# Order of the first chunks' splits, multiplies and condition groups in the prologue of a gated feed-forward kernel

## The reference

```python
scale = cond @ norm_w.T + 1.0
h = x * (scale[:, None, :] * rsqrt(mean(x * x) + 1e-6))
u = h @ up_w.T                        # 512 -> 2 * 2048
val, gate = split(u, 2)
h = val * gelu(gate)                  # exact gelu
hq = act_quant(h)                     # per row, 127 steps of its largest absolute value
wq = weight_quant(down_w)             # to -1, 0, 1 times a mean
x1 = hq @ wq.T + x
# adapter, whose two matrices depend on cond
Wd_b = Wd + 0.1 * (cond @ Wdd.T + bdd).reshape(B, 128, 512)
Wu_b = Wu + 0.1 * (cond @ Wdu.T + bdu).reshape(B, 512, 128)
out = x1 + relu(x1 @ Wd_b.T + bd) @ Wu_b.T + bu
```

## Time and profile before

| | us |
|---|---|
| median of 3 runs (lowest, highest) | 851.65 (851.64, 852.14) |
| the profiled execution's own time | 851.16 |
| its span in the trace | 849.1 |
| PE busy | 834.2 (98%) |
| DVE busy | 606.3 (71%) |
| ACT busy | 388.8 (46%) |
| POOL busy | 77.3 (9%) |

### The profile page before, as it was taken

How to read it: one execution, slowest core, us unless ns; L and a number is a source line. 1 busy time by engine, 2 the same in 40 slices (tenths; PEclk the granted TensorE clock), 3 DMA queues, 4 the chain that set the end, 5 groups by cost and what they waited for, 6 DMA issues and landing times.

```text
span 849.1 us, 11801 instructions
## 1 busy us (share of the span) xinstructions
PE 834.2 (98%) x3982; PEld 366.9 (43%) x3982; DVE 606.3 (71%) x904; ACT 388.8 (46%) x633; POOL 77.3 (9%) x79
## 2 busy tenths in 40 slices
PE   6899999999999999999999999999999999999998
PEld 4334444444444444444444444444444444444443
DVE  5998787989877765558776556668975664445986
ACT  5678887765454532237445542126433332224000
POOL 0463333302000000001000000000200000000100
PEclk9999999999999999999999999999999999999999
DMA  9879988666999843377899754436247444432232
GB/s 344 329 259 341 348 284 299 236 222 217 327 343 361 300 164 118 112 247 272 296 316 328 274 197 137 154 106 205 86 135 219 137 161 140 139 114 78 100 123 75
DMA packets 64426, 183.49 MB, mean 216 GB/s; under 512 B 7024, under 2 KB 8304, under 8 KB 64368
## 3 DMA queue, kind: packets, MB, share of 16 engines
q1 hardware_dynamic: 64080, 182.48, 61.7%
q10 hardware_dynamic: 288, 0.26, 0.1%
HBM read 152.31 MB, written 29.36 MB: 214 GB/s over the span
## 4 chain that ended last, share of the span: by engine, by line
PE 93%; DVE 1%; issue 0%; DVEq 0%
PE aux_ps L1182 10%; PE b_ps L1082 9%; PE b_ps L1084 9%; PE b_ps L1086 9%; PE a_ps L1082 6%; PE a_ps L1084 6%; PE a_ps L1086 6%; PE aux_ps L1137 6%; PE aux_ps L1233 3%; PE aux_ps L1224 3%; PE c_ps L1084 3%; PE c_ps L1082 3%; PE c_ps L1086 3%; PE e_ps L1082 3%; PE e_ps L1084 3%; PE e_ps L1086 3%
## 5 line engine op out<-in xcount | busy, mean ns | idle before, releaser
L1589 DVE SCALAR_TENSOR_TENSOR h_ring<-v_sb,unscale,gelu 128x512 f32<-128x512 f32 x63 | 51.0, 809 | 102.1 <-ACT gelu L885 54.8
L861 ACT ACTIVATE b_ps<-a_ps 128x512 f32<-128x512 f32 x63 | 36.7, 582 | 141.7 <-PE a_ps L1086 141.6
L1082 PE MATMUL b_ps<-t_mov,u_l 128*128 128x512 f16 x252 | 95.5, 379 | 0.5 <-DVE c_ps L1550 0.5
L1086 PE MATMUL b_ps<-t_mov,u_l 128*128 128x512 f16 x252 | 95.5, 379 | 0.0
L1084 PE MATMUL b_ps<-t_mov,u_l 128*128 128x512 f16 x252 | 95.5, 379 | 0.0
L1613 DVE TENSOR_TENSOR hmax<-gelu,hmax 128x512 f32<-128x512 f32 x120 | 82.8, 691 | 7.7 <-ACT gelu L891 2.6
L1182 PE MATMUL aux_ps<-h_ring,wq 128*128 128x512 f16 x384 | 84.8, 379 | 0.0
L753 POOL PARTITION_ALL_REDUCE yscale<-hmax x8 | 17.8, 2265 | 601.9 <-DVE hmax L1613 601.2
L895 ACT ACTIVATE gelu<-h_ring 128x512 f32<-128x512 f32 x64 | 40.3, 629 | 56.6 <-DVE h_ring L1589 56.6
L891 ACT ACTIVATE gelu<-h_ring 128x512 f32<-128x512 f32 x64 | 40.2, 629 | 52.5 <-DVE h_ring L1599 52.4
L1599 DVE SCALAR_TENSOR_TENSOR h_ring<-b_ps,unscale,gelu 128x512 f32<-128x512 f32 x64 | 47.9, 749 | 18.8 <-PE b_ps L1086 18.7
(11 more groups left out here) (225 smaller groups left out, 1622.1 us busy)
## 6 DMA issues: line engine op xcount, KB each, us to landing
w_ring<-in_Wdu SPq DMA_DIRECT2D x64, 512.0 KB, 6.1
w_ring<-in_Wdd SPq DMA_DIRECT2D x56, 512.0 KB, 6.7
u_l<-ul_dram SPq DMA_DIRECT2D x48, 512.0 KB, 4.6
u_e<-ue_dram SPq DMA_DIRECT2D x48, 384.0 KB, 3.1
h_ring<-in_up_w SPq DMA_DIRECT2D x16, 512.0 KB, 6.3
x_sb<-in_x SPq DMA_DIRECT2D x8, 1024.0 KB, 8.0
res<-in_down_w SPq DMA_DIRECT2D x16, 512.0 KB, 7.5
ul_dram<-u_l SPq DMA_DIRECT2D x15, 512.0 KB, 5.3
```

The source lines that it names most:

```text
L1082: pe.matmul(ps[:, :], weight(n, p, 0, k), hi, start=fresh and k == 0, stop=False, skip_group_check=True)
L1086: mm = pe.matmul(ps[:, :], weight(n, p, 1, k), hi, start=False, stop=k == 1, skip_group_check=True)
L1589: dve.scalar_tensor_tensor(out=h_slot(n)[:, TB:TS], in0=val[:, :], scalar=unscale[:, s // 2, j:j + 1], in1=gelu2[:, :], op0=ALU.mult, op1= ...
```

## The change

It changes orders and no work. No instruction and no transfer is added or taken out. The names are those above.

- ACT: the early groups' copies are interleaved otherwise. Group 0's is in front of `t_high(0, B21)`, 1 and 2 behind it, and 3 and 4 around `row_sums(3)`. `u_high(1, 0)` and `u_high(1, 1)` come in front of `t_high(0, T1)`, and `u_high(1, 2)` and `seed_b(1)` in front of `t_high(0, T3)`.
- PE: group 0 in front of `spread_rs(1)`, group 2 in front of the B21 products, groups 3 and 4 around `bounds(1, 2)`, and group 7 in front of P7 of quad 1.
- DVE: `exponents(1, 2)` and `u_scale(1)` in front of T1. T1 and T2 back to back. `u_low(1, 0)` and `u_low(1, 1)` in front of `t_low(0, T1)`. `multiply2(0)` ahead of `t_low(0, T2)` and ahead of `multiply1(0)`. `u_low(1, 2)` in front of T3, `u_low(1, 3)` in front of `t_low(0, T3)`, and `u_scale(2)` behind it. `slot_empty(0)` stays written in both multiplies of quad 0.

```diff
--- before.py
+++ after.py
@@ -935,30 +935,32 @@
             t_high(0, B11)
             u_high(0, 2)
             row_sums(2)
+            stage_group(0)
             t_high(0, B21)
-            stage_group(0)
             stage_group(1)
+            stage_group(2)
             t_high(0, B12)
             t_high(0, B22)
             gate1(0)
-            stage_group(2)
+            stage_group(3)
             row_sums(3)
-            stage_group(3)
-            t_high(0, T1)
-            t_high(0, T2)
+            stage_group(4)
             u_high(1, 0)
             u_high(1, 1)
+            t_high(0, T1)
             gate2(0)
-            stage_group(4)
+            t_high(0, T2)
             stage_group(5)
+            u_high(1, 2)
             stage_group(6)
+            seed_b(1)
             t_high(0, T3)
-            u_high(1, 2)
             u_high(1, 3)
             for n in range(1, NQ):
                 s, j = divmod(n, NP)
                 last = j == NP - 1 and s + 1 < NSB
-                seed_b(n)
+                if n > 1:
+                    seed_b(n)
                 if last:
                     t_high(s + 1, B11)
                 if j == 0:
@@ -1253,21 +1255,22 @@
             stat1(1)
             first_product(a_ps[0], True, False, B11).then_inc(s_p[1], 1)
             first_product(b_ps[0], True, True, B11).then_inc(s_p[5], 1)
+            adapter_group(0)
             spread_rs(1)
-            adapter_group(0)
             adapter_group(1)
+            adapter_group(2)
             first_product(a_ps[0], False, False, B21).then_inc(s_p[2], 1)
             first_product(b_ps[0], False, True, B21).then_inc(s_p[4], 1)
-            adapter_group(2)
             adapter_group(3)
             pe.wait_ge(s_ms, 2)
             bounds(1, 2, e_ps).then_inc(s_total, 1)
+            adapter_group(4)
             pe.wait_ge(s_xs, 2 * KD)
             first_product(c_ps, True, False, B12).then_inc(s_p[6], 1)
             first_product(b_ps[1], True, True, B12)
             first_product(c_ps, False, False, B22).then_inc(s_p[3], 1)
             first_product(b_ps[1], False, True, B22).then_inc(s_p[7], 1)
-            for g in range(4, EARLY - 1):
+            for g in range(5, EARLY - 1):
                 adapter_group(g)
             for n in range(NQ):
                 if n:
@@ -1279,9 +1282,13 @@
                     if n > 1:
                         product(n - 1, 4)
                     product(n, 2)
+                    if n == 1:
+                        for g in groups_of_quad(n):
+                            adapter_group(g)
                     product(n, 7)
-                for g in groups_of_quad(n):
-                    adapter_group(g)
+                if n > 1:
+                    for g in groups_of_quad(n):
+                        adapter_group(g)
                 if stat_of_quad(n) is not None:
                     pe.wait_ge(s_p5sb, n)
                     stat(stat_of_quad(n))
@@ -1738,22 +1745,22 @@
             x_scaled(1)
             t_low(0, B12)
             t_low(0, B22)
-            moving_sum(0, T1)
             dve.wait_ge(s_total, 1)
             exponents(1, 2, e_ps)
             u_scale(1)
+            moving_sum(0, T1)
+            moving_sum(0, T2)
+            u_low(1, 0)
+            u_low(1, 1)
+            t_low(0, T1)
+            multiply2(0)
+            t_low(0, T2)
+            u_low(1, 2)
+            moving_sum(0, T3)
+            multiply1(0)
+            u_low(1, 3)
+            t_low(0, T3)
             u_scale(2)
-            moving_sum(0, T2)
-            t_low(0, T1)
-            u_low(1, 0)
-            t_low(0, T2)
-            moving_sum(0, T3)
-            u_low(1, 1)
-            multiply1(0)
-            multiply2(0)
-            t_low(0, T3)
-            u_low(1, 2)
-            u_low(1, 3)
             aux_ready(dve, "bounds", 0)
             exponents(3, 3, bank("bounds", 0))
             u_scale(3)
```

## The result

| | median, us (lowest to highest, runs) | ratio to before, 95% interval |
|---|---|---|
| before | 850.70 (850.05 to 852.14, 20) | |
| changed | 852.62 (851.95 to 854.90, 20) | 1.0023 [1.0017, 1.0029] |
| changed, measured again (e10, before 850.92 beside it) | 852.46 (11 runs) | 1.0016 [1.0007, 1.0025] |

The change makes the kernel 1.9 us slower, 1.5 in the repetition. The forecast was 2.06 us. The median that was forecast, 853.7, is 1.1 us above the measured one, and 0.95 of that is the base: it started from the 851.65 of three runs, and 20 runs of the kernel before gave 850.70. The profiled execution of the changed kernel took 852.54 us, its span is 850.5. The profiled executions of two experiments, e5 (4150 us) and e7 (1984 us), are not used, and both kernels were measured again as e11 and e9.

The account below looks back on a forecast made before the run. DVE's queue up to `seed_c(2)` sets P7(2), and PE is the bound from there. 1.65 + 1.26 - 0.48 (old idle gone) - 0.80 + 0.45 = +2.08, by the schedule +2.06, on 851.65 gives 853.7 us; range 851.3 to 854.9.

Parts of the forecast that it names:

- The groups on PE and ACT: Early groups fill PE's idle times, P1(1) is ready at about 37.2 instead of 39.51; costed at nothing in the sum.
- Step 1: DVE up to T2: POOL's sums of chunk 2 start sooner and slow DVE less, a gain of 0.80 us (0 to 1.43).
- Step 2: DVE at `multiply2(0)`: waits for the moves of groups 0 and 1, behind tile 15, until 37.70, a wait of 1.65 us.
- Step 3: DVE at `u_low(1, 3)`: waits for ACT's `u_high(1, 3)`, which stands behind `t_high(0, T3)`, a new wait of 1.26 us.
- Step 4: DVE at low half T3: now beside POOL's sums of chunk 3 and slowed by 0.45 us (0 to 0.53).
- The first rival: PE's idle times were the bound and not DVE: 2.8 us less, end at 848.8; chance 0.08.
- the third: Rival: POOL gains nothing by its earlier start, slowing other DVE instructions as much: +2.9 us, 854.5; chance 0.15.
- The second: Rival: the moves land early, `multiply2(0)`'s wait is gone, `u_low(1, 3)`'s stays: +0.40 us, 852.05; chance 0.15.

Follow-up runs that it names:

- e10: The changed kernel measured again, nothing else changed; 852.46 us from 11 runs, +1.54 us on the kernel before (850.92 beside it), ratio 1.0016.
- e5: The kernel before with PE's and ACT's part of the change alone, DVE's order as before; ratio 1.0012 to the kernel before.
- e7: The changed kernel with group 7 behind P7(1) again; +3.0 us on the kernel before from 5 runs, measurement disturbed.
- e11: Same kernel as e5, measured again: PE's and ACT's part alone with DVE's order of before; +1.18 us on the kernel before, ratio 1.0012.
- e9: Same kernel as e7, measured again: the changed kernel with group 7 behind P7(1); +2.56 us on the kernel before, ratio 1.0029.
- e3: The changed kernel with `stage_group(0)` behind `t_high(0, B21)` again on ACT; +1.69 us on the kernel before, ratio 1.0019.
- e6: e1 with POOL's sums of chunk 2 held until group 4 is done, as late as before; +1.71 us on the kernel before, ratio 1.0019.
- e2: The changed kernel with `u_high(1, 3)` in front of `t_high(0, T3)` on ACT; +0.58 us on the kernel before, ratio 1.0005.
- e1: The changed kernel with SP's `move(1)` issued in front of tiles 14 and 15; -0.02 us on the kernel before, ratio 1.0000.
- e4: The changed kernel with the edits of e1, e2 and e3 together; +0.15 us on the kernel before, ratio 0.9999.
- e8: The changed kernel with T3, the multiplies and `seed_b(1)` moved, `stage_group(0)` as in e3; -1.07 us on the kernel before, ratio 0.9985.
- e12: e8 with POOL's sums of chunks 0 and 4 held until `seed_c(2)` is done; -2.31 us on the kernel before, ratio 0.9976.

## Why the prediction was right

**That DVE's queue sets P7(2) and P7(2) the end: right.** Every row of the table shows the second, and e11 shows that PE's and ACT's part alone loses 1.2 us.

**The groups on PE and ACT: right for P1(1)** (37.67, forecast 37.2), but group 0 was costed at nothing and is not free. In the changed kernel it was done late enough that `stage_group(0)` at 22.85 pushed `t_high(0, B21)` to 23.34, and DVE waited 0.70 instead of 0.28 for it and then took 0.27 longer beside POOL. Together 0.7 us, which the sum doesn't have. It went into the wait for the moves (e3). The order on ACT is only half of the cause: e11 has it too and waits 0.27, because in that execution the matmuls in front of group 0 got faster at 19.8 and not at 21.2 (last section).

**Step 1, POOL sooner: right in kind, too small.** 0.80 was taken, between 0 and 1.43. The durations say 1.3: the low halves B12 and B22 2.43 instead of 2.88, T1 1.21 instead of 1.75, the small one 0.17 instead of 0.51. That is all of the slowing, since e6 has the same 2.43 with no sum beside them, and the bound of 1.43 was itself 0.1 too high. I had thought that one or one and a half sums would still slow the low halves. In exchange T2 now follows directly on T1, whose result it waits for, and starts 1.32 us behind it (31.71 to 33.03) where the schedule has 1.13: 0.2 that it lacks.

**Step 2, the moves: right in place and clock time.** DVE went on at 37.69. Its wait was 1.33 by the distance of starts (1.24 in the row) instead of 1.65, because it arrived at 36.36 and not 36.05. The changed kernel's tile 15 was issued at 25.5 and landed 12.4 us later, at 37.9, which is 0.2 us after DVE had gone on. In e2 it landed at 37.7, also 0.2 after. In e3, e9 and e10 it landed at 36.9 to 37.1, 0.5 to 0.7 before. So the moves didn't land with tile 15 itself, and "behind tile 15" gave the right time to 0.1 us by more luck than the working shows. What holds DVE's start at 37.54 to 37.70 in all five profiles is not shown, only that it goes when `move(1)` is issued two tiles sooner (e1). The Trainium skill's rule that each DMA engine takes descriptors in ring order (DMA: Bandwidth & Descriptors, Queues, rings and completion order) agrees with e1. Its second half, that nothing orders the completion across engines, agrees with the two profiles in which the moves landed before tile 15. But the saving of up to 1 us in the wait, which the prediction set beside it, is in none of the five.

**Step 3, `u_low(1, 3)`: right**, 1.16 by the distance of starts (1.07 in the row) for 1.26. e2 shows that the order of two instructions on ACT is all of it.

**Step 4, low half T3 beside POOL: wrong here.** It took 1.22, and POOL's sum beside it 1.57. In e4 the same instruction in the same neighbourhood took 1.75. What differs is which starts first. In the changed kernel low half T3 starts at 43.77 and POOL's sum at 44.00, and POOL is slowed. In e4 POOL's sum starts at 42.17 and low half T3 at 42.22, and DVE is slowed (0.72 on POOL). In e1, e2, e3, e6, e9 and e10 DVE starts some 0.23 us first, as in the changed kernel, and takes 1.22 while POOL takes 1.57 or 1.58. So the later of the two gives way in all eight profiles. No run was made to test it. The step of the prediction that failed is the assumption that DVE always is the slowed one.

**The sum.** T4 moved by 1.52 and P7(2) by 1.60, for +2.06. The misses in front of the moves, 0.7 too little at B21, 0.2 too little from T1 to T2 and 0.5 too much left beside POOL in step 1, leave 0.3 to 0.4 and count for nothing, because the wait ends them all: behind it the schedule was within 0.1 us at `u_low(1, 3)` (43.11 for 43.20). The 0.45 of step 4 is most of what remains at T4. That the time (+1.92) is nearer to the forecast than T4 (+1.52) is luck: the two profiled executions differ by 1.38 (852.54 and 851.16). The first rival (PE the bound) is excluded by e11, the third (no gain from POOL) by e6. The second (moves early) is what e1 makes by hand: forecast +0.40, by the fixed point +0.38, and no change in the time. The +0.38 is right by luck as well, since nothing ends the misses there: DVE waited 1.06 us at B21, and step 1's larger gain and the absent 0.45 of step 4 made up for it.

**Group 7 in front of P7(1)** was costed at nothing. Putting it back costs 1.0 us (e9), by what its trace shows through PE's clock.

## What to carry to other kernels

Find the queue that is without gaps up to the last wait of the bounding engine. Only its idle time and its slowed instructions count, and filling the other engines' gaps in front of it brings nothing, or costs if a shared producer is pushed back. Before an instruction that overwrites a buffer is moved forward, look at which transfer empties the buffer and what stands in front of that in the transfer queue: here 37.6 us was a fixed time in all profiles with that order of transfers, whatever the engines did. Where an instruction of DVE and one of POOL meet, look at which starts first: 0.05 us decided over 0.5 us in e4. And an idle stretch that can't be removed may still be worth shortening with other work, when the clock falls behind it.

## What the hardware showed that was not expected

- Four POOL sums of 128x256 cost DVE 1.4 us when they lie beside instructions with two SBUF operands (e6), and nothing beside `x_scaled`, which reads PSUM: its four take 2.71 us in the changed kernel with POOL running beside them and 2.72 in e6 without. The Trainium skill states that contention for two SBUF inputs (GPSIMD Engine Reference, Specifications), and these traces agree. Two instructions with one SBUF tensor operand were slowed too: the 128x2 one took 0.51 instead of 0.17 us, and the first running maximum (128x512) 0.95 in e8 and 0.41 in e12, where no sum lies beside it. Moving eight sums behind `seed_c(2)` was worth another 1.2 us (e12 against e8).
- PE idle for 3.02 and 2.97 us (e9, e3) was followed by a granted clock of 0.61 and 0.57 from 46 to 49 us, 2.65 and 2.73 us (e10 and the changed kernel) by 1.00. The changed kernel itself shows a lower mean clock in 14 of its 20 timed executions, so these four rows give no border.
- In the prologue, 128x512 matmuls ran at 0.63 us each (0.43 from start to start) until 19.5 us in the kernel before and until 21.1 in the changed one, and from there at 0.38 (0.22). That is in front of PE's changed instructions. The profile gives the granted clock as 1.00 in the slow stretch too (17.0 to 19.4 us), so the 1.0 for all of the span hides it. That it is the lower of the two clock levels is read from the factor of two alone. The step comes at 19.0 us in e3 and only after 22 in e9, and group 0, `stage_group(0)` and low half B21 hang on it.
